# Encoder layers of a first attention as 64-row halves, with the order of its sines, its bias matmuls and constant matmuls changed

## What is computed

```
key_phase   = tanh(gelu(x @ Wk1 + bk1) @ Wk2 + bk2) * freq * pi
query_phase = tanh(gelu(x @ Wq1 + bq1) @ Wq2 + bq2) * freq * pi
V           = x @ Wv + bv
memory      = cumsum(exp(i * key_phase) * V, over tokens)
retrieved   = real(sum(memory * exp(-i * query_phase))) / sqrt(positions * K)
out         = x + layernorm(retrieved) @ Wo + bo
```

## Time and profile before

| | us |
|---|---|
| median of three runs | 592.09 |
| lowest, highest | 591.37, 593.07 |
| profiled execution | 588.52 |
| its span | 586.8 |
| PE busy in the span | 528.1 |
| VectorE busy | 413.1 |
| ScalarE busy | 379.0 |
| POOL busy | 17.0 |
| mean granted clock of TensorE | 0.973 of full |

### The profile page before, as it was taken

How to read it: one execution, slowest core, us unless ns; L and a number is a source line. 1 busy time by engine, 2 the same in 40 slices (tenths; PEclk the granted TensorE clock), 3 DMA queues, 4 the chain that set the end, 5 groups by cost and what they waited for, 6 DMA issues and landing times.

```text
span 586.8 us, 8247 instructions
## 1 busy us (share of the span) xinstructions
PE 528.1 (90%) x2798; PEld 292.8 (50%) x2798; DVE 413.1 (70%) x1114; ACT 379.0 (65%) x619; POOL 17.0 (3%) x29
## 2 busy tenths in 40 slices
PE   1999899999999997779999999999946999999995
PEld 1656685344433343656766666766624443434341
DVE  6877798566626666798999999999885526333334
ACT  0369748557466663448878888888834666666662
POOL 4070000000000000000000000000000000000000
PEclk9979998999999998989999999999998899999999
DMA  7900020312121223000000000000000322322221
GB/s 213 266 8 1 1 55 1 130 55 72 37 80 51 79 83 107 1 1 1 1 1 1 2 1 0 2 1 1 1 1 1 100 65 57 95 72 83 79 84 25
DMA packets 26840, 28.08 MB, mean 48 GB/s; under 512 B 12240, under 2 KB 17392, under 8 KB 26736
## 3 DMA queue, kind: packets, MB, share of 16 engines
q1 hardware_dynamic: 24496, 26.98, 15.8%
q10 hardware_dynamic: 2304, 0.58, 0.6%
HBM read 26.24 MB, written 1.31 MB: 47 GB/s over the span
## 4 chain that ended last, share of the span: by engine, by line
PE 50%; DVE 36%; issue 6%; ACT 6%; DMA 1%; SPq 0%; DVEq 0%; ACTq 0%
PE bank L1544 19%; PE bank L1555 18%; DVE l1mom L1277 3%; DVE Xs L1270 3%; PE bank L1392 2%; DVE Xn L1302 2%; DVE small L1238 2%; DVE Cen L1283 2%; DVE Mm L1263 1%; DVE ksm L1207 1%; DVE Ph L1232 1%; DVE small L1226 1%; DVE mom L898 1%; ACT Hd L770 1%; PE bank L1459 1%
## 5 line engine op out<-in xcount | busy, mean ns | idle before, releaser
L683 ACT ACTIVATE Hd<-bank,b1all 128x512 f32<-128x512 f32 x176 | 105.7, 702 | 49.8 <-PE bank L1544 49.8
L1119 DVE SCALAR_TENSOR_TENSOR Tmp<-bank,b2col,Wb 128x512 f32<-128x512 f32 x56 | 42.0, 750 | 90.2 <-PE bank L1555 89.7
L1555 PE MATMUL bank<-Hd,w2m 128*64 128x512 f32 x352 | 82.6, 600 | 1.2 <-DVE Tmp L1119 1.2
L683 ACT ACTIVATE onehot<-bank,b1all 128x512 f32<-128x512 f32 x80 | 48.7, 704 | 27.0 <-PE bank L1544 27.0
L1544 PE MATMUL bank<-XT,w1m 64*128 64x512 f32 x256 | 61.8, 616 | 0.0
L1544 PE MATMUL bank<-Ph,w1m 64*128 64x512 f32 x256 | 61.3, 614 | 0.0
L1555 PEld LDWEIGHTS bank<-Hd,w2m 128*64 128x64 f32 x352 | 23.0, 136 | 54.9 <-issue 51.9
L1544 PEld LDWEIGHTS bank<-XT,w1m 64*128 64x128 f32 x256 | 28.0, 191 | 29.9 <-issue 28.2
L1544 PEld LDWEIGHTS bank<-Ph,w1m 64*128 64x128 f32 x256 | 27.4, 190 | 29.2 <-issue 27.3
L1668 PEld LDWEIGHTS bank<-bd,XT 128*128 128x128 f32 x256 | 32.3, 198 | 17.6 <-ACT Hd L770 16.6
L770 ACT ACTIVATE Hd<-bank,lvecs 128x512 f32<-128x512 f32 x64 | 38.8, 689 | 3.5 <-PE bank L1717 3.4
(11 more groups left out here) (215 smaller groups left out, 883.2 us busy)
## 6 DMA issues: line engine op xcount, KB each, us to landing
Wb<-gate_rows SPq DMA_DIRECT2D x128, 128.0 KB, 2.9
Ph<-in_x SPq DMA_DIRECT2D x4, 512.0 KB, 8.6
Ph<-in_itok SPq DMA_DIRECT2D x4, 384.0 KB, 9.3
w1m<-in_w1e SPq DMA_DIRECT2D x1, 1028.0 KB, 17.4
w2m<-in_w2e SPq DMA_DIRECT2D x2, 512.0 KB, 12.9
w1m<-in_w1e SPq DMA_DIRECT2D x1, 1024.0 KB, 5.5
out<-Hs SPq DMA_DIRECT2D x16, 64.0 KB, 1.9
Hd<-in_w1all SPq DMA_DIRECT2D x1, 512.0 KB, 13.3
```

The source lines that it names most:

```text
L683: ac.activation(hidden_rows(st)[:, k // 2, k % 2, :], ps(("up", st.m, st.n, k))[:, :], func, bias=b1all[:, st.m, st.e, k // 2:k // 2 + 1]) ...
L1119: ve.scalar_tensor_tensor(dst, bank[st.down_bank][:, :], b2, Wb[:, st.t % RING, :], ALU.add, ALU.mult).then_inc(down_read, 1)
L1555: ins = te.matmul(bank[st.down_bank][h * D:(h + 1) * D, :], w2m[:, st.e, hc * D:(hc + 1) * D], hidden_rows(st)[:, hc, h, :], start=(hc == ...
```

## The change

The encoder weights become plain 64-row blocks; each encoder matmul uses 64 rows (one half, or one kind) in place of 128 rows of which half are zeros. In `encode2`, in the bank plan and in `tanhs` the half now is the outer loop and the kind the inner one. ScalarE runs gelus(2) before sines(0), loads the table set `silu_and_others` by name ahead of it, and runs sines(0), sines(1), tanhs(2) and sines(2) in a row; scale_weights and both retrieved copies follow sines(2). The bias matmuls move from before `xt(0, 0)` to both sides of encode2(3), and their addition on VectorE moves behind phases(3). PE multiplies constants (`ident` by `causal`, 384 columns, result never read) five times before `xt(0, 0)`, and twice each before and after encode2(2). scores(0) moves behind encode2(2). The banks change accordingly.

```
-    put("b1", (0, 6))
-    quarters("enc2", 0, 7, 1, 2, 7)
+    phases(0, 7, 1, 2, 7)          # kind is n % 2, half is n // 2
-    quarters("enc2", 1, 5, 1, 4, 7)
+    phases(1, 5, 1, 4, 7)
-    quarters("score", 0, 2, 7, 3, 2)
-    quarters("enc2", 2, 0, 7, 6, 4)
-    quarters("score", 1, 3, 2, 7, 6)
-    put("ret", (0, 1), (1, 4))
+    phases(2, 3, 7, 6, 4)
+    quarters("score", 0, 2, 1, 0, 2)
+    quarters("score", 1, 5, 1, 0, 2)
+    put("ret", (0, 0), (1, 4))
-    quarters("enc2", 3, 4, 2, 0, 3)
+    put("b1", (0, 7))
+    phases(3, 4, 2, 0, 3)
...
-        w_enc1 = sb("w_enc1", [P, 2, P])
-        w_enc2 = sb("w_enc2", [P, 2, P])
+        w_enc1 = sb("w_enc1", [P, P])
+        w_enc2 = sb("w_enc2", [P, P])
...
-            gp.memset(w_enc1[:, :, :], 0.0)
-            gp.memset(w_enc2[:, :, :], 0.0)
...
             tanhs(1)
-            sines(0)
             xt_out(0, 3)
             gelus(2)
+            ac.preload_act_table_set("silu_and_others")
+            sines(0)
             sines(1)
             tanhs(2)
+            sines(2)
             scale_weights(range(0, 4))
             retrieved(0)
-            sines(2)
             retrieved(1)
...
             phases(3)
+            bias_in()
             attended(0)
...
+            def keep_busy(key, times):
+
+                pe.wait_ge(consts_ready, 1)
+                dst = bank_free(key)
+                for _ in range(times):
+                    te.matmul(dst[:, 0:384], ident[:, :], causal[:, :], start=True, stop=True)
...
-            bias_through_w1()
...
-                    made(te.matmul(dst[:, :], w_enc1[:, h, :], gsl(XT, g), start=True, stop=True), ("enc1", g, h))
+                    made(te.matmul(dst[:, :], w_enc1[hs, :], XT[hs, gslice(g)], start=True, stop=True), ("enc1", g, h))
...
-                        made(te.matmul(dst[:, :], w_enc2[:, kind, :], Gk[:, g % 2, h, :], start=True, stop=True), key)
+                        made(te.matmul(dst[:, :], w_enc2[ks, :], Gk[ks, g % 2, h, :], start=True, stop=True), key)
...
+            keep_busy(("xt", 0, 0), 5)
             xt(0, 0, Xs)
...
             encode1(2)
+            keep_busy(("enc2", 2, 0, 0), 2)
+            encode2(2)
+            keep_busy(("score", 0, 0, 0), 2)
             scores(0)
-            encode2(2)
             scores(1)
...
             encode1(3)
+            bias_through_w1(range(0, E // 2))
             encode2(3)
+            bias_through_w1(range(E // 2, E))
             xt(1, 0, Xn)
```

More of the change, by code:

```diff
@@ L75, in quarters, with phases @@
             plan.add((what, g, n // 2, n % 2), b)
+    def phases(g, *banks):
+        for n, b in enumerate(banks):
+            plan.add(("enc2", g, n % 2, n // 2), b)
     put("table", (0, 2), (1, 3), (2, 4))
@@ L576, in _ @@
                 hs = slice(h * D, (h + 1) * D)
-                act.dma_start(w_enc1[hs, h, :], a["enc1"]).then_inc(enc_in, 16)
-                act.dma_start(w_enc2[hs, h, :], a["enc2"][h]).then_inc(enc_in, 16)
+                act.dma_start(w_enc1[hs, :], a["enc1"]).then_inc(enc_in, 16)
+                act.dma_start(w_enc2[hs, :], a["enc2"][h]).then_inc(enc_in, 16)
                 act.dma_start(bd0[hs, :, hs], a["Wvo"]).then_inc(enc_in, 16)
@@ L629, in tanhs @@
             def tanhs(g):
-                for kind in range(2):
-                    for h in range(2):
+                for h in range(2):
+                    for kind in range(2):
                         key = ("enc2", g, kind, h)
@@ L1016, in _, with bias_in @@
                 layernorm(0, u, Hs, Xs)
[L1019 to L1023, removed]
+            def bias_in():
+                dve.wait_ge(b1all_in, 16)
+                full(dve, ("b1", 0))
+                b1 = b1all[:, 0, :, :].rearrange("p e c -> p (e c)")
+                read(ve.tensor_tensor(b1, ps(("b1", 0))[:, 0:2 * E], b1, ALU.add), ("b1", 0))
             def phases(g):
@@ L1406, in _, with bias_through_w1 @@
                 made(te.matmul(dst[0:rows, 0:D], lhs, rhs[:, :], start=True, stop=True), ("table", n))
-            def bias_through_w1():
+            def bias_through_w1(experts):
                 pe.wait_ge(b1_in, 32)
                 dst = bank_free(("b1", 0))
-                for e in range(E):
+                for e in experts:
                     for hc in range(2):
@@ L1416, in bias_through_w1 @@
                                         start=True, stop=True)
-                made(ins, ("b1", 0))
+                if e == E - 1:
+                    made(ins, ("b1", 0))
+            def keep_busy(key, times):
[3 more added lines that the diff above has]
+                    te.matmul(dst[:, 0:384], ident[:, :], causal[:, :], start=True, stop=True)
             pe.wait_ge(tables_ready, 1)
@@ L1448, in encode1 @@
                 for h in range(2):
+                    hs = slice(h * D, (h + 1) * D)
                     dst = bank_free(("enc1", g, h))
-                    made(te.matmul(dst[:, :], w_enc1[:, h, :], gsl(XT, g), start=True, stop=True), ("enc1", g, h))
+                    made(te.matmul(dst[:, :], w_enc1[hs, :], XT[hs, gslice(g)], start=True, stop=True), ("enc1", g, h))
             def encode2(g):
-                for kind in range(2):
-                    for h in range(2):
+                for h in range(2):
+                    taken(pe, ("enc1", g, h))
+                    for kind in range(2):
                         key = ("enc2", g, kind, h)
+                        ks = slice(kind * D, (kind + 1) * D)
                         dst = bank_free(key)
-                        taken(pe, ("enc1", g, h))
-                        made(te.matmul(dst[:, :], w_enc2[:, kind, :], Gk[:, g % 2, h, :], start=True, stop=True), key)
+                        made(te.matmul(dst[:, :], w_enc2[ks, :], Gk[ks, g % 2, h, :], start=True, stop=True), key)
             def values(g):
```

## The result

The changed kernel takes 594.54 us (median of 18 runs, 591.76 to 596.77) against 591.75 us of the kernel before (18 runs): a ratio of 1.0057, 95% interval 1.0035 to 1.0078. It is slower by 0.57%, where 591.1 us had been forecast with an upper end of 593.6. The profiled execution took 594.8 us with a span of 593.0, against 588.5 and 586.8 before.

What follows compares the result with a forecast made beforehand. The prediction saw four queues side by side as the bound: clock, PE, POOL/VectorE, ScalarE and VectorE. Starting the experts 1.1 - 0.17, about 1.0 us, earlier gave 592.09 - 1.0 = 591.1 us, range 588.6 to 593.6.

Steps and rivals of the forecast that it cites:

- the sum: First attention up to the experts: phases(3) starts 1.1 us earlier, less 0.17 for the bias addition, about 1.0 us gained.
- the upper bound that was taken: Second phase instruction of phases(0), blocked by POOL's sums: runs from 41.67 to 46.3 us, against 44.0 unblocked.
- gives the gain back: ScalarE: sines(2) ahead of scaling and both retrieved copies; copies end at 65.8 instead of 66.4, phases(3) only 1.1 us earlier.
- The constants in the first wait: PE before the first transpose: five 384-column matmuls take 3.4 us, 25.4 to 28.8, ending before the operand at 29.3; no cost.
- the last encoder layer meets a half clock: Rival at encode2(3): half clock makes it 3.6 us instead of 1.8; 2.1 us slower, 594.2 us; chance 0.13.
- PE has waits here, so this is no saving yet: Encoder layers on 64-row halves: 2.7 us less PE work a group, 10.8 us in all, not counted as a saving.
- the rest, nothing: Two memsets fewer let ScalarE issue weight loads sooner, and SP's feed-forward loads start some 1.5 us earlier: no gain from either.
- What follows moves as a block: After the first attention, about 25 to 92 us, expert layers and linear attention only shift, so nothing there becomes shorter.

## Why the prediction was wrong

**What held.** Measured from the second normalised half (38.14 us before, 41.07 after), ScalarE's and VectorE's queues did what the sum said. The second phase instruction takes 4.33 us, near the upper bound that was taken (41.67 to 46.3). The Trainium skill, "SBUF — State Buffer", section "SBUF: two separate sides", gives the lock as the reason; the trace agrees: 4.33 us beside POOL's sums and 2.35 without them. sines(1) start at 11.7 (worked out 11.8, before 14.8), sines(2) at 22.7 (22.7), retrieved(1) end at 27.4 (27.6, before 28.3), phases(3) start at 34.2 (33.8, before 35.0), behind a wait of 0.60 us for tanhs(3), one of the signs that the prediction gave of being wrong; with full clock at the layer they start at 33.2 and 33.5. The order that "gives the gain back" was named rightly and under-priced: undone, it is worth 3 us of B, the clock at the last encoder layer included. The constants in the first wait outlasted A in the first profile (they ended at 33.9), phases(0) asked 1.4 us later for it than in the second, and phases(1) still ended 11.6 us after the second half, as in the second profile: no cost, as said.

**What failed first: the clock.** The forecast gave full clock at encode2(3) and put 0.13 on "the last encoder layer meets a half clock". In five profiles of the change's order, with small edits at the start only, that layer took 2.8 to 3.8 us and the first output projection 3.3 to 3.8. The rival's working was close to the second profile: bias half 3.4 us (it said 3.8), projection ended at 81.3 us (79.5, with the second half 1.2 us earlier). That its 594.2 us lies so near the measured 594.54 is luck in part: it put 2.1 us on this stretch, where B grew by some 1.1 in the mean, and nothing on the start. The prediction had a row that speaks for it, one-column matmuls from 25.37 us and a fall at 28.9 while they ran; the change puts half of these matmuls ahead of encode2(3). But they aren't needed for a half clock: the halves alone had it there without them, in one profile, behind a wait grown from 1.30 to 1.96 us. Nor do they bring it without a wait: with the scaling first they stand there as before, PE doesn't wait, and the layer ran at full clock in all six profiles without further constants. So the step that failed is to price thinner PE work as time that lies in waits ("PE has waits here, so this is no saving yet") and to put nothing on what it does to the clock. How much the one-column matmuls add isn't separated. From the start of phases(3) to the experts the kernel before takes 18.4 us, the changed one 20.2 and 22.0; with constants it is 18.4 to 18.7 again. B is 61.0 and 60.5 with constants, 62.8 to 65.3 (mean 63.7) without: 3 us in B, 2.0 to 2.3 us in the medians. With PE's work ahead of the layer halved and no constants there, the full clock needed a reason, not the half clock.

**What failed second: "the rest, nothing".** Without the two clears POOL's large clear begins at 5.30 us instead of 5.82, and VectorE's instruction on `mtT`, which then starts behind it, takes 1.79 us instead of 0.62 or 0.29; with two clears put back it took 0.29. The first one-hot moves from 12.12 to 13.35; with the halves alone, whose tokens were 0.24 us late, A is 30.2. Where the tokens come later still, they end last and hide this: with the clears back A was 31.96. A is 30.6 to 32.2 us in seven profiles of the new order and layout with nothing held back (the kernel before: 29.3 and 29.8). Part is chance (2 us for the same kernel), about 1 us the bulk loads; the rest is not explained. The prediction began its count at 25 us and took A as given.

**What failed third: the frame.** "What follows moves as a block" holds for one length of C, not between the two. The profile of before was one of the short kind, hence its 3.6 us below the median, which the prediction noted and carried along as a constant. Of 139 runs of the kernel before 59 lie below 590.2 us (median 588.5), the others around 592.7; none of the 18 of the changed kernel does, but with 2 to 3 us lost elsewhere its short kind would lie near 591, and its runs, 591.8 to 596.8, show no gap. Five profiles of it, counting the small edits at its start, were all of the long kind. Whether the change makes the long kind likelier isn't shown.

Together, by means of the profiles: the queues take 1.8 us off B when the clock holds (62.6 to 60.7), the half clock adds 3.0, the start 1 to 2. That leaves 2 to 3 us of loss; the medians show 2.8. This sum takes the two lengths of C to be as frequent in both kernels, which isn't shown.

## What to carry to other kernels

Ahead of each stretch that must run fast, ask what keeps PE at full clock there: a wait that costs nothing itself, behind PE work that has become thin, can double the time of the work behind it, and the cure is first to shorten the wait and only then to fill it, with no more than fits into it. In a hand-written queue, an instruction that waits long (sines(2), 6.65 us idle) belongs behind the short ready ones; here that was worth 3 us of B and, with the tokens first, made a kernel about 0.45% faster than the one before, in two series of runs. Profile a kernel twice before taking its profile as the frame: a stage that nobody edits may have two lengths.

## What was not expected of the hardware

A linear attention that no edit touched takes 233.3 or 236.7 us, in the same kernel too, with the granted clock at 0.83 or 0.66 to 0.72 between 430 and 460 us. A token transfer issued at the same place in the same program landed 2 us apart (one-hot at 24.13 and 22.14 us). Taking away two clears of 0.31 us each made another engine's instruction three times as long.
